# One fused q/k/v weight, a softmax over tile pairs, and ternary weights as two compares, in stage 1 of a two-layer network

## What is computed

```python
q = (x @ Wq + bq).reshape(B, L, GROUPS, HPG, HEAD_DIM)          # 4 groups x 8 heads x 16
kv = (x @ Wkv + bkv).reshape(B, L, GROUPS, 2, HEAD_DIM)         # 4 x (16 key + 16 value)
scores = jnp.einsum('blghd,blgd->blgh', q, k)[..., None] / math.sqrt(HEAD_DIM)
attn = jax.nn.softmax(scores, axis=-1)                           # over an axis of length 1
out = attn * v[:, :, :, None, :]
...
gamma = jnp.mean(jnp.abs(w))                                     # for each of w1, w2, w3
jnp.clip(jnp.round(w / (gamma + EPS)), -1.0, 1.0)                # -1, 0 or 1
```

## Time and profile before

| | us |
|---|---|
| median of 3 runs | 1493.93 |
| lowest, highest | 1493.19, 1500.76 |
| the profiled execution, its own time | 1492.56 |
| its span in the profile | 1490.7 |
| first matmul of the feed-forward block in it | 153.85 |

### The profile page before, as it was taken

How to read it: one execution, slowest core, us unless ns; L and a number is a source line. 1 busy time by engine, 2 the same in 40 slices (tenths; PEclk the granted TensorE clock), 3 DMA queues, 4 the chain that set the end, 5 groups by cost and what they waited for, 6 DMA issues and landing times.

```text
span 1490.7 us, 19483 instructions
## 1 busy us (share of the span) xinstructions
PE 1376.6 (92%) x7106; PEld 929.8 (62%) x7106; DVE 1041.8 (70%) x2176; ACT 657.3 (44%) x1190; POOL 699.8 (47%) x839
## 2 busy tenths in 40 slices
PE   4988999999897999999799898989999999999997
PEld 3766454444484444458444445778888888888885
DVE  3899556555486677767677775288867767887776
ACT  4654323221222455562245457455545545464442
POOL 1466302213061123555112346578668867876862
PEclk9998899999995999999699999999999999999999
DMA  9000100000046012105701200513323222333300
GB/s 360 21 1 1 55 17 29 1 1 29 1 128 170 2 44 44 58 1 183 198 2 44 72 30 29 197 57 114 139 87 142 85 85 85 144 115 134 115 31 29
DMA packets 45908, 114.78 MB, mean 77 GB/s; under 512 B 3314, under 2 KB 4339, under 8 KB 42228
## 3 DMA queue, kind: packets, MB, share of 16 engines
q1 hardware_dynamic: 44756, 112.21, 22.8%
q10 hardware_dynamic: 1056, 1.31, 0.3%
HBM read 92.28 MB, written 20.97 MB: 76 GB/s over the span
## 4 chain that ended last, share of the span: by engine, by line
PE 61%; DVE 22%; ACT 5%; DMA 4%; SPq 3%; POOL 3%; issue 2%; ACTq 0%; POOLq 0%; DVEq 0%
PE PS L1397 60%; DVE cm L482 4%; DVE SM L498 2%; DVE PS L683 2%; DVE SM L494 2%; SPq L353 2%; DMA QG<-MT 1%; PE PS L1406 1%; DVE SM L488 1%; SPq L361 1%; DVE sm L494 1%; POOL SM L1219 1%; DVE hm L491 1%; DMA qs<-qm 1%; ACT EX L1046 1%
## 5 line engine op out<-in xcount | busy, mean ns | idle before, releaser
L1219 POOL TENSOR_TENSOR SM<-SM 128x1 f32<-128x1 f32 x256 | 119.9, 472 | 326.8 <-DVE SM L488 316.6
L1046 ACT ACTIVATE EX<-PS 128x512 f32<-128x512 f32 (+3 forms) x384 | 167.3, 495 | 183.9 <-PE PS L1397 182.9
L1219 POOL TENSOR_TENSOR ws_g<-rw,ws_g 128x512 fp32r<-128x512 f32 x64 | 138.2, 2159 | 128.9 <-ACT ws_g L887 128.9
L1310 POOL TENSOR_SCALAR_AFFINE_SELECT EX<-EX 128x128 f32<-128x128 f32 x256 | 73.6, 297 | 240.4 <-ACT EX L1046 236.2
L1397 PE MATMUL PS<-KG,QG 96*128 96x512 f32 (+3 forms) x384 | 148.2, 420 | 16.2 <-DVE SM L683 12.4
L683 DVE CUSTOM_DVE_ANT_0 PS<-PS,MW 128x128 f32<-128x128 f32 (+3 forms) x256 | 121.7, 504 | 52.3 <-PE PS L1397 52.0
L1397 PE MATMUL PS<-QG,KG 98*128 98x512 f32 (+3 forms) x384 | 132.3, 386 | 19.1 <-DMA QG<-MT 17.1
L1188 ACT ACTIVATE ab<-hm 128x512 f32<-128x512 f32 x64 | 40.5, 633 | 204.6 <-DVE hm L482 204.6
L1397 PE MATMUL PS<-ws_d,HH 128*128 128x512 f32 x528 | 125.7, 389 | 0.2 <-DVE HH L482 0.2
L1397 PEld LDWEIGHTS PS<-QG,KG 98*128 98x128 f32 x384 | 71.4, 196 | 86.7 <-issue 47.5
L482 DVE TENSOR_TENSOR cm<-cm 128x512 bf16<-128x512 bf16 (+1 forms) x136 | 117.2, 892 | 2.4
(11 more groups left out here) (163 smaller groups left out, 2852.8 us busy)
## 6 DMA issues: line engine op xcount, KB each, us to landing
rw<-in_L_ffn_w_gate SPq DMA_DIRECT2D x16, 1024.0 KB, 5.1
rw<-in_L_ffn_w_up SPq DMA_DIRECT2D x16, 1024.0 KB, 5.1
rw<-in_L_ffn_w_down SPq DMA_DIRECT2D x16, 1024.0 KB, 6.9
QG<-qs SPq DMA_DIRECT2D x48, 256.0 KB, 5.4
raw<-in_L_ffn_w SPq DMA_DIRECT2D x3, 2816.0 KB, 19.3
qs<-qm SPq DMA_DIRECT2D x16, 256.0 KB, 6.7
qs<-qn SPq DMA_DIRECT2D x16, 256.0 KB, 4.3
ys<-xA SPq DMA_DIRECT2D x4, 1024.0 KB, 3.9
```

What stands on the lines that cost most here:

```text
L1046: e.activation(EX[:, n % 16, 0:W], PS[:, score_bank(n), 0:W], ACT.Exp, scale=ISQ, bias=0.0).then_inc(S["ex"], 1)
L1219: return e.tensor_tensor(out, a, b, op)
L1310: e.affine_select(out=p, in_=p, compare_op=ALU.is_ge, fill=0.0, base=0, pattern=[[1, 128]], channel_multiplier=-1).then_inc(S["sel"], 1)
```

## The change

Seven edits, all in stage 1.

1. Queries, keys and values have one weight `WQK` in two halves of 256 query and 64 key/value columns. `project1` takes 24 matmuls of 320 columns (and four for the bias) into two PSUM banks, where 12 of 512 and 12 of 128 (and two and two for the bias) stood. A projection alternates between banks 4, 5 and 6, 7.
2. The weights of the projection are loaded first: the first half of Wq and Wkv, then the second half of Wq on ACT's queue, and SP holds back tiles 1 to 3 and everything behind them until the first part has landed. The split of the weights goes by parts.
3. ACT's step 1 does the norm of tile 0 ahead of the weights. Within a step ACT does depth 5, 3, 6, then the copies of the turned blocks, then depth 1 and 9.
4. The maximum and the sum over one element are gone; difference, exponential, reciprocal and product work on two tiles at once (64 columns), in every second step; so do `o`, its statistics, its norm and the addition.
5. `quantize` makes two compares, `qa` (above) and `below` (below), both `tensor_scalar`, without a wait between them, at the end of DVE's step. PE turns a block by two matmuls that add in PSUM: `qa` with the identity `idb` and `below` with minus the identity `idn`. The turned blocks are float32 and have two banks (2, 3) where there were three.
6. PE's order: a chunk's third group of blocks opens the next step, the first two close a step. The last 14 blocks (28 matmuls) are turned in the first two turns of the feed-forward loop.
7. |w| is summed in 4 pieces of 1408 columns a matrix, where there were 11 of 512.

```diff
             e.dma_start(xA[:, 0:1, :], xin[:, 0:1, :]).then_inc(S["d_x0"], 16)
+            e.dma_start(BR[0:1, :, 0:256], bq_d.rearrange("(a h n) -> a h n", a=1, h=2)).then_inc(S["d_b"], 16)
+            e.dma_start(BR[0:1, :, 256:320], bkv_d.rearrange("(a h n) -> a h n", a=1, h=2)).then_inc(S["d_b"], 16)
+
+            w.wait_ge(S["d_wqa"], 32)
             e.dma_start(xA[:, 1:4, :], xin[:, 1:4, :]).then_inc(S["d_x1"], 16)
...
-                w.wait_ge(S["dvs"], did(ts1(qa[:, 0:n], src, gone[m][:, 2:3], ALU.is_gt)))
-                stt(qbc[c % 2][:, 0:n], src, gone[m][:, 3:4], qa[:, 0:n], ALU.is_lt, ALU.subtract).then_inc(S["qm"], 1)
+                ts1(qa[c % 2][:, 0:n], raw[m][:, s:s + n], gone[m][:, 2:3], ALU.is_gt)
+                ts1(below(c)[:, 0:n], raw[m][:, s:s + n], gone[m][:, 3:4], ALU.is_lt).then_inc(S["qm"], 1)
...
-                w.wait_ge(S["dvs"], did(red(m[:, 0, :], pr[:, i % 2, :].rearrange("p (n d) -> p n d", d=16), ALU.add)))
-                w.wait_ge(S["dvs"], did(red(m[:, 1, :], m[:, 0, :].rearrange("p (n d) -> p n d", d=1), ALU.max)))
-                tt(m[:, 2, :], m[:, 0, :], m[:, 1, :], ALU.subtract).then_inc(S["sd"], 1)
+                n = did(red(m[:, 0, 32 * x:32 * x + 32], pr[:, i % 2, :].rearrange("p (n d) -> p n d", d=16), ALU.add))
+                if x:
+
+                    w.wait_ge(S["dvs"], n)
+                    tt(m[:, 1, :], m[:, 0, :], m[:, 0, :], ALU.subtract).then_inc(S["sd"], 1)
...
-                w.wait_ge(S["dvs"], did(red(m[:, 4, :], m[:, 3, :].rearrange("p (n d) -> p n d", d=1), ALU.add)))
-                w.wait_ge(S["dvs"], did(e.reciprocal(m[:, 5, :], m[:, 4, :])))
-                tt(m[:, 5, :], m[:, 5, :], m[:, 3, :], ALU.mult).then_inc(S["at"], 1)
+                w.wait_ge(S["dvs"], did(e.reciprocal(m[:, 3, :], m[:, 2, :])))
+                tt(m[:, 3, :], m[:, 3, :], m[:, 2, :], ALU.mult).then_inc(S["at"], 1)
...
+                phase1(s)
                 if 0 <= s - 9 < 12:
                     quantize(s - 9)
-                phase1(s)
...
         def turn_bank(t):
-            return (2, 3, 7)[turn_no[t] % 3]
+            return 2 + turn_no[t] % 2
...
+                        mm(out, qa[c % 2][:, sl], idb[:, :], True, False)
+                        last = mm(out, below(c)[:, sl], idn[:, :], False, True)
...
+                out = [PS[:, 4 + 2 * (i % 2) + a, 0:320] for a in range(2)]
...
+                    for x, hl in ((xh, 0), (xh, 1), (xl, 0)):
+                        for a in range(2):
+                            last = mm(out[a], x[:, c], WQK[:, hl, c, a, :], False, c == 3 and x is xl)
...
+                if n == 0:
+                    quantized(10, 2)
+                    quantized(11, 0)
+                if n == 1:
+                    quantized(11, 1)
+                    quantized(11, 2)
```

More of the change, by code:

```diff
@@ L100, in col @@
             return stat[:, 6 * n + k:6 * n + k + w]
-        gsum = [small(NH) for _ in range(3)]
+        gsum = [small(4) for _ in range(3)]
         gone = [small(4) for _ in range(3)]
@@ L191, in network @@
         turns = []
-        for s in range(22):
+        for s in range(23):
             turns += [("s", (s - 8) // 4)] if s in (8, 12, 16) else []
-            turns += [("t", gdone[s - 10] + k) for k in range(groups[s - 10])] if 0 <= s - 10 < 12 else []
+            turns += [("t", gdone[s - 11] + 2)] if 0 <= s - 11 < 12 and groups[s - 11] == 3 else []
+            turns += [("t", gdone[s - 10] + k) for k in range(2)] if 0 <= s - 10 < 12 else []
         turn_no = {t: n for n, t in enumerate(turns)}
         def turn_bank(t):
-            return (2, 3, 7)[turn_no[t] % 3]
+            return 2 + turn_no[t] % 2
+        sums = [(s, m, k) for m in range(3) for k, s in enumerate((5, 5, 6, 6) if m == 0 else range(4 * m + 3, 4 * m + 7))]
         jobs = [("q", c) for c in range(4)] + [("ld", 0), ("k", 0), ("v", 0)] + [("c", c) for c in range(4)]
@@ new lines, in phase1 @@
+                if 3 in at_k:
+                    i = at_k[3]
+                    w.wait_ge(S["tp1"], i + 1)
+                    w.wait_ge(S["kp"], max(0, i - 1))
+                    split_hi(i % 2, xT1[:, i % 2, 0], 1.0, "hi1")
+                if 6 in at_k and at_k[6] % 2:
+                    p = at_k[6] // 2
+                    w.wait_ge(S["sd"], p + 1)
+                    e.activation(sm1[:, p % 2, 2, :], sm1[:, p % 2, 1, :], ACT.Exp, scale=0.25, bias=0.0).then_inc(
+                        S["ex1"], 1)
@@ L926, in phase1 @@
+                if step < 21:
+                    quantized(step - 10, 0)
+                if 1 in at_k:
+                    i = at_k[1]
+                    w.wait_ge(S["rs1"], i + 1)
+                    w.wait_ge(S["tp1"], max(0, i - 1))
+                    norm(xn1[:, i % 2, :], xt(i), i).then_inc(S["xn1"], 1)
+                if 9 in at_k and at_k[9] % 2:
+                    for i in (at_k[9] - 1, at_k[9]):
                         w.wait_ge(S["rs2"], i + 1)
                         w.wait_ge(S["x1"], max(0, i - 1))
-                        norm(yn1[:, i % 2, :], o0[:, i % 3, :], 16 + i).then_inc(S["yn1"], 1)
@@ L1464, in pe_program @@
                         project1(i)
+                for k, i in stages(NT, 11, s):
                     if k == 2:
```

256 lines of the change are left out of this document (131 added, 125 removed).

## The result

| | before | after |
|---|---|---|
| median of the runs of this comparison, us | 1495.48 (4 runs) | 1474.36 (4 runs) |
| lowest, highest | 1493.19, 1500.76 | 1471.07, 1476.44 |
| the profiled execution, its own time (span) | 1492.56 (1490.7) | 1471.07 (1468.4) |
| first projection's first matmul | 23.13 | 15.76 |
| first feed-forward matmul | 153.85 | 129.34 |

The ratio is 0.9852, with a 95% interval of 0.9817 to 0.9887: 1.5% faster, about 21 us. Predicted were 1476 us and a range of 1468 to 1485. Where the time comes from is read at the marks in the last three lines: 7.4 us at the start, 24.5 where the feed-forward block starts, 23.9 where the `QW` matmuls start. Everything that was gained was gained in stage 1.

What follows compares the result with a forecast made beforehand. In stage 1 PE was taken to bound first, DVE once quantize begins. Terms -7.1 - 4.2 - 6.6 - 2.7 + 2.9 = -17.7 took 1492.56 to 1474.9; with 1.4 for the median, 1476 us, range 1468 to 1485.

Steps and rivals of the forecast that it cites:

- 1. The start: Start of stage 1: first projection at 16.0 us instead of 23.13, -7.1 us, bounds 15 and 19.
- Tiles 1 to 3 and w1 competed: At the start: the first weights, 0.75 MB without these competing loads where 1.25 MB competed, land at about 6 us.
- tiles 1 to 3 come late: Rival at the start: tiles land late behind the weights, start at 19, 3 us less gain, 1479; chance 0.08.
- 2. Steps without ternary work: Early stage 1 projection steps: 5.15 us each instead of 5.92, between 4.6 and 5.9; -4.2 us.
- the line: Projection matmuls: a line through 512- and 128-column costs gives 0.171 us for 320 columns; 3.8 for 24 was taken midway.
- 3. Ternary steps: Ten stage 1 steps with ternary work: 7.2 us each, 72 for 78.6 in all, -6.6 us; bounds -12 and 0.
- PE becomes the pace, not DVE: Steps with ternary work: PE needs 6.85 us a step, DVE 6.4; as forecast, at about 7.2, chance 0.56.
- 7.9 a step: Rival in ternary steps: a loop over ACT, in order with two banks, replaces DVE as limit; 1483; chance 0.17.
- 0.116 a turn: Rival in ternary steps: turns cost up to a float32 matmul's 0.116 us, not 0.067; up to 10 us less, 1486; chance 0.05.
- a clock that falls inside the steps: Rival in ternary steps: bank waits drop PE's clock to 1.2 GHz, 9.9 us a step, 1503; chance 0.03.
- 4. The way out: Last projection's end to first feed-forward matmul: 10.8 us where 13.44 stood, -2.7 us.
- 5. The turns in the feed-forward loop: Feed-forward loop: 28 turns at 0.067, 1.9 us, plus about 1 us waiting for copy and sigmoid; +2.9 us.

Runs made afterwards that it cites:

- e1: Changed kernel, but SP no longer waits for the weights' first part before loading tiles 1 to 3, w1 and the rest; 1469.8 us, ratio to before 0.9844.
- e12: As e8, but with the first loads in the order of the kernel before, Wq in one piece; 1472.95 us, one run.
- e8: As e1, but both parts of the weights are awaited together before the split; 1474.65 us, one run.
- e11: Changed kernel with three idle 512-column ACTIVATEs put ahead of ACT's first xT; 1473.01 us, one run.
- e9: Changed kernel with the projection again as 12 matmuls of 512 and 12 of 128 columns, each with its bias; 1482.1 us, ratio to before 0.9909.
- e3: Changed kernel with the old two-tensor second compare, waiting for the first, and one turning matmul per block; 1478.24 us, ratio to before 0.9901.
- e10: Changed kernel with the maximum and sum over one element back, on pairs of tiles, each with its wait; 1475.04 us, ratio to before 0.985.
- e4: Changed kernel without the idn matmul, so one turning matmul per block and weights missing their -1; 1470.88 us, ratio to before 0.9859.
- e7: Changed kernel with the compares at the start of DVE's step, ahead of phase1; 1471.86 us, ratio to before 0.9848.
- e6: Changed kernel with the last 28 turning matmuls and their copies ahead of the feed-forward loop again; 1473.26 us, ratio to before 0.9851.

## Why the prediction came out, and where its steps were wrong

The total was right to 2 us, and in good part by luck. The change itself was forecast at -17.7 and came out at -21.1; the median of before was 1.5 us higher in this comparison, which hides part of that. And errors cancel: between the start and the feed-forward block the steps (2 and 3 together) came out 7.6 us shorter than I said and the way out 4.1 longer.

**1. The start: 16.0 predicted, 15.76 measured.** "Tiles 1 to 3 and w1 competed" put the cause in what SP is kept from doing. The hold is worth 0.8 at most (e1). The rest is order and pieces: the loads' order 3.5 (e12 to e8; single runs, with a landing that differs by 2), the sums of |w| moved away from the first `xT` 1.8 (1.6 in e11), and the smaller pieces of the split 1.2 (DVE is done 4.77 us after ACT's first piece in e12, 6.01 before; read from the traces, not tried apart). Together these are 7.3 of 7.4. The sum came out because it was built forward along the new order (DVE free at 12, measured 11.60); what failed is the reason that it gave for the weights' landing, as far as it lay in the tiles and w1, and it gave the sums of |w| no part in the start. The rival "tiles 1 to 3 come late" did not occur.

**2. Steps without ternary work: 5.15 predicted, 4.95 measured.** A 320-column matmul costs 0.151 (24 in 3.63 from start to start), nearer to proportion (0.142) than to the line (0.171). The mechanism stands: e9 has 5.95 in the old shape. (The sum of this step was rounded down: five times 0.77 and 0.6 are 4.45, not 4.2.)

**3. Ternary steps: 7.2 predicted, 6.83 measured, and "PE becomes the pace, not DVE" failed.** It holds for three steps only (19.77 of 20.6 us); after that DVE has 42.55 of 44. PE needs less than I said: 4.95, turns at 0.056 for my 0.067, so 4.95 + 1.2 + 0.24 = 6.4 for 6.85. Its timeline says 6.6, with the matmuls for the mean of |w| and small gaps in it: the nine steps' 61.43 us less the 1.87 that it waits for DVE. DVE needs more: my 6.4 had the second compare at 1.04, and it is 1.28 in the mean (1.82 in the even steps, while POOL makes `o`; 0.8 too much in the shorter chunks as well); the lines of the window from 50 to 125 show it with `qa` beside it:

```profile
L503 DVE TENSOR_SCALAR qb<-raw,SM 128x1536 bf16<-128x1536 f32 x6 | 7.7, 1283 | 0.0
...
L503 DVE TENSOR_SCALAR qa<-raw,SM 128x1536 bf16<-128x1536 f32 x6 | 6.1, 1011 | 0.0
```

That makes 6.6, and in the chain of waits, which from 74 on is all DVE, `qa` recurs every 6.63 us (six steps, from 78.92 to 118.69). So the two were nearly level, and the term that decided was the second compare, mis-sized by 0.24 a step through an overlap that the forecast did not have. The runs bear it out: more DVE work costs (e3 +7.3, e10 +1.75), less PE work gains nothing (e4 -0.3, with the clock as said there), more PE work costs 0.69 of each 1.0 (e9). Taken back one by one, the parts come to more than stage 1 gained behind the second projection (9.4 and 7.3 alone are more than its 16.2): with two engines nearly level, each saving counts only beside the other. The pairing of tiles by itself was not tried. There was also a miscount: seven projections stand ahead of the first turn, not six, and nine behind it, since a chunk's first groups now close a step where they opened one. Steps 2 and 3 together gave 106.2 us: 9.07 less 0.6 for the first step, five of 5.15 and ten of 7.2. Measured were 98.7 (15.76 to 114.42, where the last projection's matmuls end). Of the 7.6 less, 2.05 is the miscount (7.2 less 5.15), 1.7 the early steps, and 3.8 the nine late ones (60.97, from 53.45, for 64.8). The rivals of 7.9 a step, of 0.116 a turn and of a clock that falls inside the steps did not occur; the granted clock is 1.00 up to 118.

At the turns the Trainium skill's rule of about 81 ns for a matmul of 128 columns in a stream of loads and matmuls (TensorE: Matmul & The Clock Gate, Back-to-back issue gap) is not what these rows have: pairs that add in PSUM stand 0.056 apart (53.45, 53.50), each with its load. The measurement decides. By the page's figure a step of 21.4 turns would be 0.5 us longer on PE, an estimate, and that would have mattered a little: e9 shows that what PE gets beyond some 0.3 a step costs time.

**4. The way out: 10.8 predicted (its terms add to 10.9), 14.9 measured** (114.42 to 129.34). The larger part follows from 3: I let DVE be level with PE there. As DVE paces, it is behind when PE's last projection ends, and PE waits 4.24 for `qb`. In e9, where PE paces, the same stretch is 12.1 (127.03 to 139.16), so 2.8 of the 4.1 are DVE's lag. The other 1.3 remain there too: my list of DVE's work left out the statistics of two tiles of `o`, 2.1 us from 116.47 to 118.61 in after, ahead of the compares. The 4.1 missed here take back half of the 7.6 won in 2 and 3.

**5. The turns in the feed-forward loop: +2.9 predicted.** From the block's start to the first `w3q` matmul it is 10.81, before it was 9.84 (163.69 less 153.85): +1.0. The 28 turns at 0.056 are 1.6 and the wait 0.82, but the clock, low in both at the block's start, was back after fewer matmuls (8 in 3.24 and then 8 in 1.89, where before both eights took over 3 us). That differs between runs of the same loop: in e1, e7, e8 and e11 the clock is back later (in e1 at 134) and the distance is 12.4 to 12.6, so +2.5 to +2.8, near the forecast. e6 says that the move as a whole is worth nothing.

In sum: -20.6 predicted at the feed-forward block and -17.7 behind it; -24.5 measured at the block and -23.9 at `QW`, of which the profiled executions show -21.5 at the end and the medians -21.1. The 2.4 between `QW` and the end are within what profiles differ by there: from `QW` to the end of the span it is 1068.2 us before, 1069.8 after, and 1066.6 (e1) to 1073.2 (e10) in the runs, in none of which that part is edited; 0.8 lies outside the span.

## What to carry to other kernels

When two engines need nearly the same time for a step, the busy share and the sum of durations don't say which one paces; take work from each in turn and see which removal moves the mark, and read the granted clock of each such run: the engine that was relieved can run slower (e4). Count each stage's steps in the instruction order, not in the loop's indices, and measure small gains at marks inside the profile, since the total is less sharp than they are. At a kernel's start look at which load is last and what is queued ahead of it: the smallest load of the weights was last here, and new order and parts of the first loads together were worth 3.6 us.
